# A scan's last input period re-ordered, its first projections over three banks, and a running sum that opens with a product and is added to D·u by GpSimd's transfers

## The reference

```python
# 1. differential attention on x: 16 query heads, 8 key/value heads, head size 128, causal
p = softmax(q1 k1^T * scale) - lam * softmax(q2 k2^T * scale)
o = rms_norm(p v) * subln_w * (1 - LAMBDA_INIT);  attn = o @ out_w.T + out_b
# 2. selective scan on ctx (d_inner 512, 16 states, rank 16)
u  = silu(causal_conv(in_proj(ctx)));   dt_low, B, C = x_proj(u)
dt = softplus(dt_proj(dt_low) + dt_proj_b);   A = -exp(A_log)
state = state * exp(dt * A) + (dt * u) * B    # per channel, state and token
y  = sum over the 16 states of state * C
y  = (y + D * u) * silu(z)                    # z is the normalised stream, transposed
# 3. layer norms around each part; then experts: 16 routed (top 8), a shared one
```

## Time and profile before

| | us |
|---|---|
| median of 3 runs | 1661.8 (1660.62 to 1667.61) |
| profiled execution, its own time | 1659.59 |
| span of that execution's records | 1657.0 |
| busy: TensorE matmuls / VectorE / GpSimd / ScalarE | 1433.2 / 1312.2 / 1247.6 / 1043.7 |

### The profile page before, as it was taken

The page is one execution under the profiler, slowest core; times in us unless marked ns, Lnnn a source line. Parts: engine busy times, 40 slices in busy tenths (PEclk is TensorE's granted clock), DMA queues, the critical chain, the costliest instruction groups (busy, mean ns, idle before and its releaser), DMA issues.

```text
span 1657.0 us, 23284 instructions
## 1 busy us (share of the span) xinstructions
PE 1433.2 (86%) x7632; PEld 1150.1 (69%) x7632; DVE 1312.2 (79%) x2375; ACT 1043.7 (63%) x2407; POOL 1247.6 (75%) x613
## 2 busy tenths in 40 slices
PE   4555689999989999989999999997478999898996
PEld 1113578878868878868877878876265687676784
DVE  3996588899888899888899888887547768487575
ACT  3995366666656666656666656665347757577474
POOL 1344199999899999999999899999557448166263
PEclk9766889999999999999999999998588999899998
DMA  4466614434623433633443632424342122122021
GB/s 164 166 218 223 204 57 128 136 93 141 226 74 125 136 115 128 223 102 109 128 150 100 215 112 86 125 73 142 119 131 86 33 97 66 38 89 70 27 71 58
DMA packets 122817, 198.23 MB, mean 120 GB/s; under 512 B 10868, under 2 KB 60536, under 8 KB 121160
## 3 DMA queue, kind: packets, MB, share of 16 engines
q1 hardware_dynamic: 122696, 196.75, 37.0%
HBM read 150.18 MB, written 46.53 MB: 119 GB/s over the span
## 4 chain that ended last, share of the span: by engine, by line
PE 37%; DVE 23%; POOL 17%; issue 13%; ACT 6%; DMA 2%; SPq 1%; POOLq 0%; DVEq 0%; ACTq 0%
PE banks L589 9%; PE banks L590 8%; PE banks L591 8%; POOL act_buf L1908 5%; POOL state L1237 4%; POOL state L1254 4%; DVE state L1151 4%; PE banks L1452 2%; PE banks L1454 2%; PE banks L1453 2%; DVE banks L443 2%; DVE banks L414 1%; DVE ow_lo L1060 1%; DVE banks L1966 1%; DVE w_lo L1055 1%
## 5 line engine op out<-in xcount | busy, mean ns | idle before, releaser
L1254 POOL TENSOR_TENSOR state<-state,Cn 128x1024 f32<-128x1024 f32 x128 | 311.1, 2430 | 52.9 <-DVE state L1151 52.6
L1260 POOL TENSOR_TENSOR y_sb<-y_sb,state 128x1024 f32<-128x1024 f32 x128 | 307.5, 2402 | 21.5 <-DMA y_sb<-scratch_y 11.1
L1151 DVE TENSOR_TENSOR_SCAN state<-banks,state 128x512 f32<-128x512 f32 x256 | 310.8, 1214 | 3.4 <-ACT banks L973 2.2
L1237 POOL TENSOR_TENSOR state<-dtu_sb,Bn 128x1024 f32<-128x1024 f32 x128 | 313.2, 2448 | 0.1
L1908 POOL TENSOR_TENSOR act_buf<-act_buf,wb 128x512 f32<-128x512 f32 x128 | 165.4, 1294 | 171.4 <-ACT act_buf L1808 169.6
L973 ACT ACTIVATE banks<-dt_sb,negA 128x512 f32<-128x512 f32 x256 | 177.4, 693 | 116.8 <-DVE state L1151 115.9
L589 PE MATMUL banks<-x_hi,w_hi 128*128 128x512 f32 (+1 forms) x512 | 189.2, 369 | 38.4 <-DVE qT_lo L1081 25.2
L591 PE MATMUL banks<-x_hi,w_lo 128*128 128x512 f32 (+1 forms) x512 | 178.7, 349 | 0.0
L590 PE MATMUL banks<-x_lo,w_hi 128*128 128x512 f32 (+1 forms) x512 | 178.6, 349 | 0.0
L589 PEld LDWEIGHTS banks<-x_hi,w_hi 128*128 128x128 f32 x512 | 101.8, 199 | 58.8 <-DVE qT_lo L1081 30.7
L1956 DVE TENSOR_TENSOR hid_lo<-banks,hid_hi 128x512 fp32r<-128x512 f32 x136 | 93.8, 689 | 54.5 <-ACT hid_hi L1820 52.5
(11 more groups left out here) (217 smaller groups left out, 4440.7 us busy)
## 6 DMA issues: line engine op xcount, KB each, us to landing
x_hi<-scratch_xs SPq DMA_DIRECT2D x32, 512.0 KB, 4.8
x_lo<-scratch_xs SPq DMA_DIRECT2D x32, 512.0 KB, 6.0
Bn<-scratch_bc SPq DMA_DIRECT2D x64, 256.0 KB, 4.0
Cn<-scratch_bc SPq DMA_DIRECT2D x64, 256.0 KB, 3.4
scratch_acc<-acc_sb SPq DMA_DIRECT2D x64, 256.0 KB, 2.1
wb<-scratch_wT SPq DMA_DIRECT2D x64, 256.0 KB, 3.2
acc_sb<-scratch_acc SPq DMA_DIRECT2D x48, 256.0 KB, 3.0
w_stage<-in_w SPq DMA_DIRECT2D x32, 256.0 KB, 3.6
```

Source lines behind the costliest of these rows:

```text
L1151: nc.vector.tensor_tensor_scan(row, dA[:, :], row, 0.0, ALU.mult, ALU.add) \
L1237: nc.gpsimd.tensor_tensor(st[:, k % 4], dtu[:, 2 * h:2 * h + 2, :], Bn[:, state % NB, :].unsqueeze(1).broadcast_to([P, 2, T]), ALU.mult).t ...
L1254: nc.gpsimd.tensor_tensor(st[:, k % 4], st[:, k % 4], Cn[:, state % NB, :].unsqueeze(1).broadcast_to([P, 2, T]), ALU.mult).then_inc(S["gat ...
L1260: nc.gpsimd.tensor_tensor(y[:, 2 * h:2 * h + 2, :], y[:, 2 * h:2 * h + 2, :], st[:, k % 4], ALU.add).then_inc(S["piece_done"], 1)
```

## The change

Two independent parts.

**The last periods of the scan inputs.** SyncE now loads batch 0's dt, dtu and the first two C rows at the end of period 2 (six transfers), ahead of x, the weight stages and the biases; B's rows stay in period 4. VectorE scales the biases and `subln` in period 3, between `silu` and `softplus`, where it waits for their loads. In period 4 ScalarE squares the first half right after `guess`; the weight stages and projections follow, and stage 6 is loaded after the last stores. The first seven projections take the PSUM banks 4, 5 and 6 in turn, so a projection waits for the one three before it, not for the last.

**The sum.** In a batch's first round the product with C is written straight into `y` (no add, no load of D·u). After the last round of each half, GpSimd itself issues a DMA that adds `y` to D·u in DRAM. SyncE's eight loads and eight stores of y are gone, and the waits for them.

```diff
@@ scan_inputs, sync @@
             elif p == B:
-                ahead["scan"](sp, S)
+                ahead["rows"](sp, S)
...
-                ahead["sync"](sp, S, range(2, 5))
+                ahead["sync"](sp, S, range(2, 4))
...
-                    ahead["sync"](sp, S, range(5, 7))
+                    ahead["sync"](sp, S, range(4, 6))
...
+            if p == 2:
+                ahead["scan"](sp, S)
@@ scan_inputs, scalar @@
             if p == B:
-                ahead["scalar"](act, S, (), range(0, 1))
-                ahead["scalar"](act, S, range(2, 3), range(1, 2))
-                ahead["scalar"](act, S, range(3, 4), ())
+                square(p - 1, 0)
+                ahead["scalar"](act, S, range(2, 3), range(0, 2))
...
             square(p - 1, 1)
             if p == B:
-                ahead["scalar"](act, S, range(5, 6), range(3, 4))
+                ahead["scalar"](act, S, range(3, 4), range(2, 3))
+                ahead["scalar"](act, S, range(4, 5), range(3, 4))
+                ahead["scalar"](act, S, range(5, 6), ())
@@ scan_inputs, vector @@
-                ahead["vector"](dve, S, (), range(0, 1))
-                ahead["vector"](dve, S, range(2, 4), range(1, 2))
+                ahead["vector"](dve, S, range(2, 3), range(0, 1))
             silu(p, 0)
             silu(p, 1)
+            if p == B - 1:
+                ahead["scaled"](dve)
             softplus(p - 1, 0)
             if p == B:
-                ahead["vector"](dve, S, range(4, 5), range(2, 3))
+                ahead["vector"](dve, S, range(3, 4), range(1, 2))
             softplus(p - 1, 1)
-        ahead["vector"](dve, S, range(5, 6), range(3, 4))
+        ahead["vector"](dve, S, range(4, 5), range(2, 3))
@@ attend_and_scan @@
+    def proj_bank(r):
+        return banks[:, 4 + r % 3 if r < AHEAD else 4, :]
...
-            if r > 0:
+            if r >= AHEAD:
                 pe.wait_ge(S["proj_lo"], r)
+            elif r >= 3:
+                pe.wait_ge(S["proj_lo"], r - 2)
@@ attend_and_scan, gpsimd @@
-            if k >= 4:
-                pool.wait_ge(S["piece_done"], k - 3)
+            if k >= 4 and (k - 4) // 2 % NS == 0:
+                pool.wait_ge(S["gated"], k - 3)
+            elif k >= 4:
+                pool.wait_ge(S["piece_done"], added(k - 4))
...
+            if r == 0:
+                if b > 0:
+                    pool.wait_ge(S[f"y_added{h}"], 16 * b)
+                to = y[:, 2 * h:2 * h + 2, :]
+            else:
+                to = st[:, k % 4]
...
             if k + 3 < NDRIVE:
                 drive(k + 3)
+            if r == NS - 1:
+                pool.wait_ge(S["piece_done"], added(k))
+                nc.gpsimd.dma_start(d["y"][b][:, 2 * h * T:2 * (h + 1) * T], half(y, h), accum_op=ALU.add) \
+                    .then_inc(S[f"y_added{h}"], 16)
```

More of the change, by code:

```diff
@@ L995, in scalar @@
         for n in range(6, 8):
+            start(n)
             proj_high(n - 2)
-            start(n)
         decay(0)
@@ L1176, in vector @@
             return
-        for n in range(6, 8):
+        for n in range(5, 8):
+            start(n)
             proj_low(n - 2)
-            start(n)
         dve.wait_ge(F["bc_stored"], 16 * B)
@@ L1647, in first_loads @@
         sp.dma_start(rbias[:, :], d["route_b"].broadcast_to([P, NE])).then_inc(S["rows_loaded"], 16)
+        for h in range(2):
+            sp.wait_ge(A[f"y_added{h}"], 16)
         load_y(sp, 0)
@@ L1836, in scalar @@
         act.wait_ge(A["acc_done"], NM)
-        act.wait_ge(A["piece_done"], NDRIVE)
-        act.wait_ge(A["y_stored"], 32 * B)
+        for n in range(2):
+            act.wait_ge(A[f"y_added{n}"], 16 * B)
         for n in range(2):
```

85 lines of the change are left out of this document (36 added, 49 removed).

## The result

The changed kernel takes 1646.78 us (median of 8 runs, 1643.92 to 1654.55) against 1661.21 us of the kernel before (8 runs, 1658.08 to 1667.61): a ratio of 0.9917, 95% interval 0.9899 to 0.9934. Run again later, beside another 17 runs of before, it gave 0.9911 (0.9892 to 0.9931). So it is faster by 14.4 us where 4.6 were forecast. The profiled execution has a span of 1642.5 us, before 1657.0.

A forecast was written before the change was run, and what follows sets the result against it. TensorE was taken to pace the undisturbed stretches, with GpSimd nearly tied. Start +1.5, boundaries -3.0, last drive -0.6 and first expert split -2.5 gave -4.6 us, from 1661.8 to 1657.2 us, range 1647 to 1671.

The forecast's parts named there:

- early biases: Rival at the front: biases land early, VectorE waits 3.8 us, loop starts at most 6 us early; 1649.7 us, chance 0.18.
- Who paces: Middle phase: TensorE fills the undisturbed stretches of 16 scans, which stay at 56.9 us; GpSimd's 12 us of slack count nothing there.
- The rival with GpSimd as the pacer: Rival in the middle phase: GpSimd's removed adds and waits count in full, -18 to -27 us, about 1638; chance 0.10.
- The group boundaries: Three changes of weight group: VectorE's splits shorter beside idle GpSimd, 3 us saved; bounds 17 us saved, 4 us lost.
- The end, -3.1 us: End of scan and start of expert phase: 0.6 us for the last drive, 2.5 us for ScalarE's first split, together 3.1 saved.
- The 0.6 us for the last drive: At the scan's end VectorE no longer waits 0.6 us for GpSimd's last drive.
- The start, +1.5 us: Front: most of the wait for the biases is absorbed; the main loop starts 1.5 us later.
- projection 6 near 189: Sign at the front: projection 6, waiting for weight stage 7, begins at 189.2 us instead of 187.71.
- The wait before the bias scaling: Period 3: six moved loads, 7.7 us at 342 GB/s, delay the biases to 133.0; VectorE waits 11.4 us.
- I count them at nothing: Front: the three projection banks gain nothing, covered by VectorE's softplus; worth up to 5 us without it.
- GpSimd's transfers: The sum: eight DMA issues by GpSimd at about 1.5 us each, and waits for landing taken as 3 x 2 us.
- The dear-transfer rival: Rival in the sum: GpSimd is held 9.6 us per transfer, 26 us short over eight; 1683 us, chance 0.07.

The follow-up runs named there:

- the biases first: Changed kernel with the loads of qk_bias, subln and v_bias moved ahead of weight stage 0 in SyncE's queue; 1651.3 us.
- the sum alone: Kernel before with only the new sum (GpSimd's accumulating transfers), old front order and single projection bank; 1656.5 us.
- the front alone: Kernel before with only the re-ordered last periods and three projection banks, old sum; 1660.7 us.
- the plain store: Changed kernel with y stored plainly by SyncE at the old queue places, no GpSimd transfers, D times u missing from the output; 1647.3 us.
- the last kernel: Changed kernel with bias loads ahead of weight stage 0, GpSimd waits for both pairs of output-weight splits, seven idle-time matmuls ahead of projection 6; 1637.6 us.
- one gate: Changed kernel with one more GpSimd wait per group boundary, until VectorE has split the first two tiles of output weights; 1646.4 us.

## Why the prediction was right, and where it wasn't

**The number.** The forecast was 1657.2 us, 4.6 less, with 0.54 for a time that can't be told from before and 0.30 for a faster one (below 1653.5). It came out three times as far down, 1646.8, practically on the lower end of the range, 1647. That end stood for early biases with a part of the boundary bound. The biases weren't early enough for it; the boundaries gave 9.4 us, and 4.9 us came from eve stretches of which the forecast knew nothing. That the time still met the range's end is in part luck.

**Who paces.** Right. Undisturbed stretches stayed at 56.9 us in every kernel, whatever was done to GpSimd, and 1.6 us more of TensorE's work made one 1.6 us longer. The rival with GpSimd as the pacer would have shortened them; it didn't happen.

**The group boundaries: the term that was mis-sized.** The step was "I take 1 us saved at each of three, 3 us", with bounds of 17 us saved and 4 lost. The mechanism was right and is shown now from both sides: a gate that only delays GpSimd makes the splits short, an added wait or added work makes them long, and y's stores in SyncE's queue make no difference. The term measured 9.4 us in the profiled pair, 3.1 a boundary. Three times 5.7 us "too much" was in the text; taking a sixth of it for want of a phase was the error. (Three times the first boundary was itself too much: the pairs of the other two were 5.0 and 4.2 us too long, 14.9 in all.) The phase could have been read: before, in the first boundary stretch GpSimd's product with C at 451.41 began 6.8 us behind its scans and the next one, at 458.68 and beside the first pair, 5.6 us; after, the same two begin 3.8 and 0.1 us behind (447.97 and 452.81). The removed add and wait are 2.4 and 4.1 us.

**The end, -3.1 us: failed.** "GpSimd's own transfers go out at about 1155 and are down before" held (issued at 1139.4 and 1145.4, down by 1151.1), and the acc store became the releaser. But the step took the acc sum for unmoved relative to the scans. GpSimd's last add began 7.7 us behind the last scan before and 9.0 us after, and now a wait for it and the issue of a transfer follow, so that the adds to `x_work` begin 12.3 us behind the last scan instead of 10.1. The statistics wait 3.28 us for them, and the acc sum stands behind the statistics. 0.3 us came out. Moving two adds to VectorE didn't mend it. The 0.6 us for the last drive went the wrong way as well: VectorE waited 1.6 us for it (1.4 in the second trace).

**The start, +1.5 us.** It came out at +1.1 us in the two traces, but by luck: errors that cancel and an offset. The sign named for it, projection 6 near 189, failed: it began at 187.3, 0.4 us earlier than before, and what follows up to the first scan took 1.5 us longer at the lower clock. The last batch's first softplus began at 159.7 us, where 161 was forecast, and the last weight stages, not the softplus, set the start. The wait before the bias scaling was 7.56 us, not 11.4: the moved loads cost the queue less than their bytes at 342 GB/s (`subln`'s load is issued 17.2 us behind the store of `dtu` at 108.81; before it was 13.6 behind the one at 106.22, so 3.6 us for the 7.7 forecast). Corrected for the earlier part that no edit touches, the new front is 0.9 to 1.5 us faster than the old one. The rival of early biases was put to the test by the biases first: the first scan comes 7.1 to 7.8 us earlier, where it said at most 6. "I count them at nothing", of the three banks, was wrong: they are worth some 14 us. The step looked at projections 1 to 3 on TensorE alone. What they hold up under the new order is `u_skip` behind them in ScalarE's queue, and behind its store in SyncE's the last weight stages. So the two halves of the front edit are one: the order alone would have lost what the sum gained.

**GpSimd's transfers.** 0.87 us an issue (1.5 taken) and 3.9 us of waits in three (6 taken in all), and neither is on any path. The dear-transfer rival, 1683, has nothing left.

**What the forecast had no term for.** The eve stretches: 4.9 us of the difference between the two traces. They are the collision of the boundaries at another place, with a W_lo split and a drive that begin within 0.2 us of each other once the clock has fallen in the stretch before. The change doesn't set which comes first there: after a fall the drive was first in two of two cases before and in none of two in the changed kernel's first trace, by 0.10 us or less each way. So these 4.9 us can't be counted as the change's; nor can the 9.6 us that the trace of the sum alone lost in its three.
This is as far as the traces go. In the timed executions the sum alone gave -0.33%, the front alone nothing, both together -0.83 and -0.89%; that the two parts help each other isn't shown, since long eve stretches can hide the sum's gain, and how many there were in the executions without a trace isn't known. The mean clock of an execution doesn't tell: eight of 13 of the changed kernel have 0.936 or above against none of 20 of the two parts alone, but the kernel with the plain store, as fast and with the same stretches, has none of six. Why the same 1.8 us of idle TensorE brings the clock down in 17 of 39 cases and not in the others stays open; so does whether the filler or the changed phase kept it up in the last kernel, since the two weren't tried apart.

## What to carry to other kernels

An operation of VectorE with two operands in SBUF beside a busy GpSimd costs up to a whole GpSimd operation more: here up to 2.9 us instead of 0.7, beside operations of 2.4. Which of the two pays is decided by which begins first, and 0.1 us can decide over 1.4 to 3.7 us of the kernel's time. If such operations are few and on the path, and GpSimd isn't the pacer, hold GpSimd for them with a wait. Gate every neighbour too, because a freed operation comes earlier and meets the next one: one gate gave nothing (189.7 us for the three boundary stretches, 187.9 without it), both gates with the filler took them from the 189.1 of the biases first to 178.8 us.
Measure such a change by stretches between fixed instructions, not only by the end: here the same stretch repeats to 0.1 to 0.3 us as long as the same instruction comes first, while single executions differ by 21. Where such a stretch has two lengths, look for two instructions that change places.
When an order is changed, look for the single buffer that the old order hid: one bank cost 14 us here.

## What the runs showed of the hardware

The granted clock fell to half (0.50 over two microseconds) behind an idle time of 1.8 us in some executions and stayed at 1.00 behind the same idle time in others, with the same instructions on both sides. A fall costs little by itself where TensorE has short waits behind it that take it up (seven eve stretches of 57.9 us with a fall in the stretch before, where those without one take 57.8 to 57.9); it cost 1.4 to 3.7 us where it shifted a split behind a drive. A gain of some microseconds early in the kernel can be lost that way: the biases first gained 7 us at the first scan and lost 8.6 in three such stretches.
An accumulating transfer of 0.5 MB issued by GpSimd took it 0.87 us and landed after 5.6 to 7.9 us. The Trainium skill, page "SBUF — State Buffer", section "SBUF: two separate sides", warns that such a transfer can starve while VectorE holds the shared port pair. No issue here was held noticeably, the longest took 1.04 us; but none of the eight was issued beside a split, only beside scans and short operations, so these runs don't put the warning to the test.
